# A graph network on one core: last edge tiles handed over singly, logit tiles in two loads, unit weights loaded ahead of a scatter, middle biases inside the products

## The reference, cut to what matters

```python
x = x + L0_gnn(layernorm(x))     # two GATv2 convolutions, 8 heads and 1 head
x = x + L0_ffn(layernorm(x))     # mixture of 8 experts, top 2, 768 -> 3072 -> 768
x = x + L1_gnn(layernorm(x))     # two GAT layers
x = x + L1_ffn(layernorm(x))     # quantised two-layer block
x = x + L2_gnn(layernorm(x))     # graph convolution
x = x + L2_ffn(layernorm(x))     # mixture of 6 experts, top 2, 768 -> 96 -> 768
x = x + L3_gnn(layernorm(x))     # two GAT layers
x = x + L3_ffn(layernorm(x))     # mixture of 8 experts, top 2, 768 -> 768

# GATv2, twice in L0_gnn
e = leaky_relu(fs[src] + fd[dst], 0.2)
logits = einsum('ehd,hd->eh', e, attn)
# then a softmax over the edges of one dst, and a sum of alpha * fs[src]

# L2_ffn
topk_weights = softmax(top_k(xf @ gate_w + gate_b, 2))
hmid = gelu(einsum('nh,ehf->nef', xf, w1) + b1)
expert_out = einsum('nef,efh->neh', hmid, w2) + b2      # then the weighted sum of the chosen two
```

## Time and profile before

| what | value |
|---|---|
| median of three timed runs | 2988.08 us (2979.14 to 2998.24) |
| profiled execution, its time | 2978.18 us |
| profiled execution, span from first to last instruction | 2976.4 us |
| mean granted TensorE clock | 0.913 of full speed |
| busy share of the span | PE 84%, DVE 72%, ACT 46%, POOL 26% |

### The profile page before, as it was taken

How to read it: one execution, slowest core, us unless ns; L and a number is a source line. 1 busy time by engine, 2 the same in 40 slices (tenths; PEclk the granted TensorE clock), 3 DMA queues, 4 the chain that set the end, 5 groups by cost and what they waited for, 6 DMA issues and landing times.

```text
span 2976.4 us, 41464 instructions
## 1 busy us (share of the span) xinstructions
PE 2504.5 (84%) x12635; PEld 1998.8 (67%) x12636; DVE 2157.5 (72%) x4356; ACT 1362.8 (46%) x2651; POOL 760.6 (26%) x939
## 2 busy tenths in 40 slices
PE   5979999966999966588999999958986888898695
PEld 2536666656599954477999999944854544577495
DVE  7988888888467646689877878865967334677485
ACT  0026666655077741267656656621912110335273
POOL 4958888820056641100000000020001000000102
PEclk8979999987999977699999999978997979899698
DMA  9801111053033320577666647650010110100596
GB/s 312 266 24 31 31 31 31 29 136 125 8 45 50 51 34 1 173 256 268 214 224 219 226 167 259 231 195 25 1 62 6 56 24 1 48 17 1 177 419 254
DMA packets 83611, 351.82 MB, mean 118 GB/s; under 512 B 26984, under 2 KB 27421, under 8 KB 75950
## 3 DMA queue, kind: packets, MB, share of 16 engines
q1 hardware_dynamic: 56772, 300.70, 31.3%
q0 software_dynamic: 26656, 48.90, 5.2%
HBM read 292.28 MB, written 57.23 MB: 117 GB/s over the span
## 4 chain that ended last, share of the span: by engine, by line
PE 60%; DVE 18%; DMA 7%; POOL 6%; issue 5%; ACT 4%; SPq 0%; POOLq 0%; DVEq 0%; ACTq 0%
PE PS L856 15%; PE PS L946 10%; PE PS L1090 6%; PE PS L993 6%; PE PS L1092 3%; POOL logits L734 3%; DMA NEG<-in_L_ffn_expert_w 2%; PE PS L979 2%; PE PS L1109 2%; PE PS L1111 2%; PE PS L1110 2%; DVE w1s L2229 1%; PE PS L1180 1%; DVE w2s L2234 1%; POOL F L722 1%
## 5 line engine op out<-in xcount | busy, mean ns | idle before, releaser
L856 PE MATMUL PS<-large_rows,turned 125*128 x1448 | 527.4, 367 | 39.0 <-issue 18.4
L856 PE MATMUL PS<-small_rows,turned 125*128 x1448 | 492.3, 343 | 0.0
L734 POOL DMA_INDIRECT logits<-lgr,key x362 | 361.7, 999 | 247.2 <-DVE lgr L1836 177.3
L946 PE MATMUL PS<-WB,XT 128*125 128x384 f32 (+1 forms) x1120 | 390.2, 508 | 0.0
L1090 PE MATMUL PS<-urowsT,w1s 128*128 128x384 f32 (+2 forms) x1164 | 354.2, 369 | 32.6 <-DVE F L2242 20.9
L856 PEld LDWEIGHTS PS<-large_rows,turned 125*128 125x128 f32 x1448 | 272.8, 188 | 87.0 <-issue 75.0
L946 PEld LDWEIGHTS PS<-WB,XT 128*125 128x125 f32 x1120 | 213.5, 193 | 161.1 <-issue 36.9
L1092 PE MATMUL PS<-urowsT,w1s 128*128 128x192 f32 (+2 forms) x1164 | 297.5, 256 | 0.0
L993 PE MATMUL PS<-F,PT 125*125 125x96 f32 (+3 forms) x1500 | 280.8, 338 | 19.2 <-ACT PT L1418 8.2
L856 PEld LDWEIGHTS PS<-small_rows,turned 125*128 125x128 f32 x1448 | 272.3, 188 | 8.0
L1090 PEld LDWEIGHTS PS<-urowsT,w1s 128*128 128x128 f32 x1164 | 221.7, 190 | 57.8 <-DVE F L2242 28.5
(11 more groups left out here) (371 smaller groups left out, 5121.0 us busy)
## 6 DMA issues: line engine op xcount, KB each, us to landing
XN<-in_L_ffn_w SPq DMA_DIRECT2D x98, 769.0 KB, 4.4
PB<-in_L_ffn_w SPq DMA_DIRECT2D x97, 768.0 KB, 5.5
WB<-node_ids SPq DMA_DIRECT2D x44, 512.0 KB
logits<-NEG SPq DMA_DIRECT2D x8, 1367.2 KB
WB<-logits SPq DMA_DIRECT2D x5, 2187.5 KB
C<-in_L_ffn_expert_w SPq DMA_DIRECT2D x9, 1152.0 KB, 9.1
NEG<-in_L_ffn_expert_w SPq DMA_DIRECT2D x9, 1152.0 KB, 10.1
slot_rows<-NEG POOLq DMA_DIRECT2D x13, 768.0 KB, 57.5
```

Of the source, the lines that this page charges most:

```text
L734: pool.indirect_dma_start(out=table, out_offset=bass.IndirectOffsetOnAxis(ap=key[:, i:i + 1], axis=0), in_=lgr[:, i % EU, 0:HEADS[g]["h"]] ...
L856: mm = pe.matmul(out, ohT[i % 3][:, (1 - side) * P:(2 - side) * P], part[side][:, bass.ds(c, 1), a:b].rearrange("p o n -> p (o n)"), start ...
L946: mm = pe.matmul(PS[0:R, 4 + g % 4, 0:hw], XT[:, k, t * R:(t + 1) * R], w[:, k, half * hw:(half + 1) * hw], start=(k == 0), stop=(k == kc ...
```

## The change

It has four parts. (A) In both edge stages the last nine tiles (from LONE = 172 on) pass through `finish` one by one instead of four at a time, and POOL's scatters from tile 173 on wait for their own tile. (B) In stage 1 SP holds the load of logit tile 1 until tile 0 has landed; in stage 2 logit tile 0 is a load of its own, and tiles 1 to 4 follow it as a second one. (C) In the last mixture the fourth weight buffer is the second part of XTz instead of XN, and unit 1's weights are issued ahead of the wait for the row scatter. (D) In the middle mixture `mix_bias(1)` is gone; the biases b2 are loaded as a 97th row under w2, and the hidden values get a 97th row of ones, set by a DVE memset ahead of the graph layer before. PE's order becomes first(0), wait for `comb`, and then for each expert first(e+1), wait for GELU, expert_out(e).

```diff
+ROUTER_LOADS = (3, 5, 8)
+LONE = ES - 9
...
+def logit_group(i):
+    return i // 4 if i < LONE else LONE // 4 + i - LONE
...
-               XTz[:, 0:G3], XN[:, :, :].rearrange("p t d -> p (t d)")[:, 0:G3]]
+               XTz[:, 0:G3], XTz[:, G3:2 * G3]]
...
                         if t == 1:
                             sp.wait_ge(s_whole, T)
+                            sp.wait_ge(s_lt[0], 32)
...
-                    in_two(lambda a, b: ltile1[a:b], lambda a, b: tiles[a:b], s_lt[1])
+                    in_two(lambda a, b: ltile1[a:b, 0:1], lambda a, b: tiles[a:b, 0:1], s_lt[0])
+                    in_two(lambda a, b: ltile1[a:b, 1:T], lambda a, b: tiles[a:b, 1:T], s_lt[1])
...
             sp.dma_start(Fz[0:96, 0:4608], ins["L2_ffn_w2"]).then_inc(s_m2w, 16)
+            sp.dma_start(Fz[96:97, 0:4608], ins["L2_ffn_b2"].rearrange("(o e) d -> o (e d)", o=1)).then_inc(s_m2w, 16)
...
             square_weights(0)
+            square_weights(1)
             sp.wait_ge(s_scr, 2 * 16 * 2 * T)
             square_rows(0)
-            square_weights(1)
...
-                if i % 4 == 0:
-                    pool.wait_ge(s_lg, -(-ES // 4) * g + i // 4 + 1)
+                if i % 4 == 0 or i > LONE:
+                    pool.wait_ge(s_lg, (logit_group(ES - 1) + 1) * g + logit_group(i) + 1)
...
-                w2 = Fz[0:96, 0:4608].rearrange("p (e d) -> p e d", e=6)
-                hT = Oz[0:96, 0:2 * N].rearrange("p (u n) -> p u n", u=2)
-                pe.wait_ge(s_m2w, 48)
-                for e in range(6):
+                w2 = Fz[0:97, 0:4608].rearrange("p (e d) -> p e d", e=6)
+                hT = Oz[0:97, 0:2 * N].rearrange("p (u n) -> p u n", u=2)
+                pe.wait_ge(s_m2w, 64)
+
+                def first(e):
...
+                first(0)
+                pe.wait_ge(s_comb, 2)
+                for e in range(6):
+                    if e + 1 < 6:
+                        first(e + 1)
                     pe.wait_ge(s_mg, 2 * e + 2)
...
             route(1, 7)
-            mix_bias(1)
-            pe.wait_ge(s_mixd, 2 * T)
             mixture1()
...
-                a, n = i // 4 * 4 % EU, i % 4 + 1
+                n = i % 4 + 1 if i < LONE else 1
+                a = (i + 1 - n) % EU
...
-                    if i % 4 == 0 and i:
+                    if i and (i % 4 == 0 or i > LONE):
                         finish(0, i - 1)
...
+            link(dve.memset(Oz[96:97, 0:2 * N], 1.0))
             attend(4, onto_x=True)
...
             route(1)
-            mix_bias(1)
             mixture1()
```

More of the change, by code:

```diff
@@ L475, in build @@
                    ("L3_ffn_router_w", "L3_ffn_router_b")]
-        MIXB = ["L0_ffn_b2", "L2_ffn_b2", "L3_ffn_expert_b"]
+        MIXB = ["L0_ffn_b2", None, "L3_ffn_expert_b"]
         N_EXP = [8, 6, 8]
@@ L538, in router @@
                 if n:
-                    sp.wait_ge(s_mixp, T * n)
                     sp.wait_ge(s_comb, n)
@@ L542, in router @@
                 sp.dma_start(rb[:, 0:N_EXP[n]], ins[ROUTERS[n][1]].to_broadcast([R, N_EXP[n]])).then_inc(s_rw, 16)
-                sp.dma_start(mixb[0:N_EXP[n], :], ins[MIXB[n]]).then_inc(s_rw, 16)
+                if n != 1:
+                    wait(sp, s_mixp, T * (n // 2))
+                    sp.dma_start(mixb[0:N_EXP[n], :], ins[MIXB[n]]).then_inc(s_rw, 16)
             in_two(lambda a, b: X[a:b], lambda a, b: ins["x"].rearrange("(t p) d -> p t d", p=R)[a:b], s_x)
@@ L1017, in route @@
                 e = N_EXP[n]
-                pe.wait_ge(s_rw, 48 * (n + 1))
+                pe.wait_ge(s_rw, 16 * ROUTER_LOADS[n])
                 for t in range(T):
@@ L1032, in mix_bias @@
                 tr.then_inc(s_mbt, 1)
-                pe.wait_ge(s_mbc, n + 1)
+                pe.wait_ge(s_mbc, n // 2 + 1)
                 for t in range(T):
-                    g = T * n + t
+                    g = T * (n // 2) + t
                     wait(pe, s_mixd, g - 1)
@@ L1301, in _ @@
             mix_bias(2)
-            pe.wait_ge(s_mixd, 3 * T)
+            pe.wait_ge(s_mixd, 2 * T)
             mixture2()
@@ L1440, in mix_bias @@
             def mix_bias(n):
-                act.wait_ge(s_mbt, n + 1)
+                act.wait_ge(s_mbt, n // 2 + 1)
                 act.copy(AT[0:8], PSz[0:8, 0:T * P].rearrange("h (t n) -> h t n", t=T)[:, :, 0:R])\
@@ L1517, in mixture1 @@
                 hT = Oz[0:96, 0:2 * N].rearrange("p (u n) -> p u n", u=2)
-                act.wait_ge(s_m2w, 48)
+                act.wait_ge(s_m2w, 64)
                 for e in range(6):
@@ L1536, in round_weights @@
                         act.wait_ge(s_mb, MB3 + 2 * (u - 2) + half + 1)
-                    act.wait_ge(s_m3w[2 * (u % 2) + half], 96 * (u % 2) + 16 * (u // 2 + 1))
+                    act.wait_ge(s_m3w[2 * (u % 2) + half], (128 - 32 * half) * (u % 2) + 16 * (u // 2 + 1))
                     act.copy(w3s[:, 2 * (u % 2) + half, 0, :], uw3[2 * (u % 2) + half]).then_inc(s_h3, 1)
@@ L1832, in finish @@
                 for k in range(n):
-                    last = i // 4 * 4 + k - EU
+                    last = i + 1 - n + k - EU
                     if last >= 0:
@@ L1920, in front @@
                         else:
-                            dve.wait_ge(s_lt[1], 32 * 3)
+                            dve.wait_ge(s_lt[min(t, 1)], 32 * 4 if t == 0 else 32 * 3)
                             src = ltile1[:, t, :]
@@ L2066, in route @@
                 dve.wait_ge(s_rtp, n + 1)
-                dve.wait_ge(s_rw, 48 * (n + 1))
+                dve.wait_ge(s_rw, 16 * ROUTER_LOADS[n])
                 if e < 8:
@@ L2109, in mix_bias @@
                                       ALU.add).then_inc(s_mixd, 1)
-                dve.wait_ge(s_mixd, T * (n + 1))
+                dve.wait_ge(s_mixd, T * (n // 2 + 1))
             def add_expert(done, t, parity, e, measure=False):
```

## The result

The changed kernel took 2962.34 us (median of 6 runs, 2960.05 to 2965.83) against 2989.46 us for the kernel before (6 runs): a ratio of 0.9915 with an interval of 0.9898 to 0.9933, or 25.4 us (20 to 30.5). The forecast was 30.9 us and 2957 us; the time lies in the range. The gain is 4.5 us short of the 29.9 us (1%) from which on the prediction would have called it faster.

What follows compares the result with a forecast made beforehand. No single engine was taken to bound the kernel (PE held 60% of the chain). D 26.4, A and B 2.65 and 1.2, C 0.6 summed to 30.9 us off the median 2988.1, giving 2957 us; range 2940 to 2973.

Steps and rivals of the forecast that it cites:

- the start of first(0): Middle mixture: first(0) directly behind the routing starts at about 2414.8 instead of 2437.56, 22.75 us earlier.
- rival 1: Middle mixture: the clock rises later, first(0) and most of first(1) run low, 4 to 6 us of D lost; 2962, chance 0.15.
- the interleaving: Middle mixture: first(e+1) covers PE's wait for GELU, 0.61 us for each of six experts, 3.7 us in all.
- the same tail gives 2503.6: Middle mixture's end: XN starts 13.79 us behind the start of the last expert's products, as before, so at 2503.6.
- for 2.65: Edge stage 1: 2.15 us from earlier scatters (A) plus 0.5 from loading tile 0 alone (B).
- for 1.2: Edge stage 2: 0.9 us from POOL's shorter waits (A) plus 0.3 from the split logit load (B).
- +0.3: Edge stage 2: B's net gain from starting tile 0 ahead of tiles 1 to 4, ends -0.6 and 1.2 us.
- Rival 3: Edge stages: the tails don't shrink, A and B give 0 instead of 3.85 us; 2961, chance 0.10.
- I take 2.7: Last mixture: unit 1's weights slow the row scatter's landing by 2.7 us, ends 0 and 5.6.
- Rival 2: Last mixture: the weights crowd the scatter, so C gives -2.3 us and not +0.6; 2960, chance 0.12.
- the base of 12.37 us: First mixture: the scatter's landing with no weights beside it, set against 15.10 us in the last mixture with unit 0's.
- Rival 4: Middle mixture: the clock fallen during routing does not rise at all, costing 76.7 us; 3034, chance 0.04.

Runs made afterwards that it cites:

- the fillers: The change without C plus identity products on PE: 22 behind the last expert's products (2946.46 us, 0.9894), then 14 more ahead of the last routing's transposes (2942.46 us, 0.9880).
- B alone: The kernel before with only the order and cut of the logit loads changed in both edge stages: 2978.15 us, ratio 1.0002.
- one run (10.9): The change without C, with unit 0's weights too issued only behind the row scatter and first row load: 2951.57 us, ratio 0.9904.

## Why the prediction came out as it did

**D, the start of first(0)**: right. The order without interleaving takes 23.2 us from the stretch (115.2 to 92.0), for 22.75 forecast. The bias row held nothing up, the wait for `comb` was free, the memset of ones took 1.10 us on DVE but next to nothing of the path (PE's last 200 products ahead of the routing took 72.2 to 72.3 us with it and 72.0 to 72.2 without, where the clock was alike), and rival 1 did not happen.

**D, the interleaving**: sized too low in the stretch (5.3 us for 3.7), and the sum lacked a term behind it. The prediction stopped at XN, "the same tail gives 2503.6". But what follows the tail is not the same. In the kernel before the clock had fallen ahead of XN, in PE's waits for DVE between the last products; with interleaving PE comes into these waits without the last wait for GELU, the clock falls some 5 us later, and is low for longer behind XN, where PE works. It is low again at a row of transposes and at the last routing's, where it was full before: over the whole stretch the mean granted clock is 0.90 instead of 0.93. That gives back 4.9 us of the 5.3. Without interleaving this loss is gone, and the fillers show that it is the clock: the first returns 3.7 us and the second 3.0 more, at places where the clock is then full. Why the clock falls in two later waits of one kernel, and not in the same waits of the other (2.10 us, and 3.56 and 3.57 us at the last routing), is not settled.

**A and B**: the mechanism was right, the sizes were too low. Stage 1 gained 3.2 us (20.95 to 17.75, means over all profiles) for 2.65. Stage 2 gained 3.5 (29.8 to 26.4) for 1.2; mis-sized is the term "+0.3" for B there, which measured 2.6 in the one run of B alone (the ten runs with A and B spread from 24.8 to 28.3). The front and the turn of tile 0 lie ahead of the other tiles' landing, and those landed 8.01 us behind their own issue, where all five took 9.87; over all profiles it is 7.6 to 8.5 us in eleven with B and 9.0 to 9.9 in three without. Tile 1 was not late in stage 1. Rival 3 did not happen.

**C**: the step that failed is "I take 2.7" for the slowing of the scatter. 4.1 us were lost, and 2.3 gained for 3.3, so that C costs 1.9 us (standard error 0.9) where it was to give 0.6. Rival 2 happened, at nearly its price (2.3). The 2.7 rested on two landings of one profile each, in two mixtures, and on the second 2.36 MB costing what the first did. The landing with one unit's weights spreads from 12.7 to 16.9 us, so that these two could not give the price; whether the base of 12.37 us was wrong as well rests on one run (10.9). By the Trainium skill ("DMA: Bandwidth & Descriptors", section "Queues, rings and completion order") a DMA engine takes turns between the queue rows that have work, a packet from one and then from the next. The runs fit that: the second 2.36 MB cost the scatter 4.1 us, three quarters of the 5.5 us that they take at 426 GB/s, and halfway between the prediction's 2.7 and 5.6.

**The sum** by the stretches: 28.6 - 4.9 + 3.2 + 3.5 - 1.9 = 28.5 us. The change measured 25.4 (20 to 30.5) the first time and 28.9 (24 to 34) the second. That the forecast of 30.9 came so near is in part luck: A, B and D in the stretch gave 5 us more than their terms, and the 4.9 us behind XN and C's 2.5 us took 7 away. Rival 4 did not happen, since the clock did rise in the mixture; what the clock took lies behind the mixture, where no rival looked.

## What to carry to other kernels

A step that removes waits moves the wait to the next place, so read on past the point where the gain is counted: here an order of products gained 5.3 us and the next layer gave 4.9 back; unused filler products in two waits of TensorE took 6.7 us out of that layer again. A load that is brought forward over a scatter slows the scatter; price it from several profiles of the same scatter with and without the load, not from one profile of another scatter. With gains of 2 to 5 us in 3000, compare stretches between named instructions over several profiles: those on PE agreed to 0.1 us, where totals moved by 10; the landing of a scatter moved by 4.

## What the runs showed of the hardware

The last routing's transposes and its narrow products (8 columns) took 5.09 and 9.51 us at a low clock (0.66 in the mean over the transposes) and 3.53 and 7.93 at a higher one, decided by filler in the 3.6 us ahead of them. The granted clock can fall although PE is recorded busy: with two fillers PE was busy for 7.00 of 7.00 us in the last routing, and the clock fell there (0.82 in the mean), as it did in the middle routing. The clock's course behind the mixture repeated from execution to execution: seven runs agree on the 237.7 us to 0.1 us, although their mixtures ended up to 10 us apart. Ahead of the mixture it did not: the middle routing's products took 7.9 to 8.1 us in six profiles and 9.5 to 9.6 in eight, with or without part D. A second load of 2.36 MB beside an indirect scatter of 3.85 MB delayed its landing by 4.1 us; the first by 2 to 4, as the base is taken.
